# Two graph-attention layers on one core: fewer signals from TensorE, a second set of PSUM banks, deeper rings

## The chip, the core and the metric

One NeuronCore of a Trainium2 chip runs the whole program. The metric is the device time in microseconds, from the start to the end of one execution. The engines are named as in the profile: PE (TensorE matmul; PEld its weight loads), DVE (VectorE), ACT (ScalarE), POOL (GpSimd) and SP (SyncE, which here only issues DMAs). Each runs its own instruction stream, and they wait for each other through semaphores. A "signal" below is an increment of a semaphore that an instruction makes when it completes.

## What is computed

A graph of 6,250 nodes with 128 features and 106,250 edges (100,000 and a loop on each node), sorted by destination. Layer 0 scores each edge by a dot product, layer 1 by an 8-head attention with edge features. What matters of the reference:

```python
# layer 0
qk = x @ Wqk + bqk;  v = x @ Wv + bv
scores = clip(sum(qk[dst] * qk[src], -1) / sqrt(D), -5, 5)
attn = softmax of scores over the edges of one dst
out = segment_sum(attn * v[src], dst) @ Wo + bo      # then residual and norms
# layer 1
z = leaky_relu(xl[src] + xr[dst] + edge_attr @ lin_edge_w.T, 0.2)
alpha = softmax of einsum('ehc,hc->eh', z, att) over the edges of one dst
attn_out = segment_sum(xl[src] * alpha, dst)         # then residual, MLP, norms
```

## The kernel before, in words

The edges are cut into 832 tiles of 128 edges. Four tiles are a quad (208 quads), four quads a group (52 groups). Since edges are sorted by destination, the destinations of a tile lie in a window of 128 consecutive nodes. A gather (a DMA that POOL issues with one row index per edge) fetches the source rows, SP loads the window of the destination table, and one-hot matrices, made by comparing index vectors, spread and collect rows by matmul.

**Layer 0, per quad Q.** SP loads the four windows of `p_tab` and one row of relative indices (`rel_bc`), L253 and L255, into one of SLOTS = 4 slots. POOL issues four gathers (L279) into one of AHEAD0 = 4 slots. DVE makes the one-hot matrix `spread` (L538, ring of 2). PE spreads the window rows in two halves (`spread_p(Q, k)`, L320, two tiles each, into `p_dst0` and `p_dst1`). DVE multiplies them with the gathered rows (`score(Q, k)`, L548) and clips (L566). ACT makes the exponential and the weighted one-hot matrix `gather1` (`weigh`, L438 to L446, ring of 2). PE forms the weighted sums of rows and weights (`add_up(Q, k)`, L330 and L332, two halves, into `tile_sums0` and `tile_sums1`), and DVE adds each tile to `node_sums` (`add_tile`, L560).

The order on each engine is written out by hand. In step T the PE does `spread_p(T+1, 0)`, `add_up(T-1, 0)`, `spread_p(T+1, 1)`, `add_up(T-1, 1)`. Each half ends in a signal of its own: `p_spread` after a half of the spreading, `summed` after a half of the sums, so four in a quad. DVE does `make_spread(T+1)`, then for each half `score(T, k)` and two `add_tile` of quad T-2, then `clip(T)`. SP waits for `p_spread` of quad Q-4 before it loads quad Q, POOL waits for `summed` of quad Q-4 before it gathers quad Q. A PE half waits until DVE has read the same bank of the quad just before (`scored`, `added`). In the first 13 quads the PE also makes blocks of `p_tab` (`make_p`, banks `lr_ps`). From step 204 on the node-wise part of the layer runs beside the last quads (`project`, `turn_y`, `tables`; banks `o_ps`, `t_ps`, `lr_ps`). That is eight PSUM banks in all.

**Layer 1, per quad Q.** SP loads four windows of `xr_tab` (L830), and for each group 1 MB of edge features and the indices. POOL gathers four tiles of `xl_tab` (L846) after it waits for `z_ready` of quad Q-4. PE builds z in one bank (`make_z`): edge features times weights (L905), spread windows (L909), gathered rows (L913), signal `z_ready`. ACT reads it twice (`split_z`, L857 and L858), after waits for `z_ready` and for `lg_ready` of two quads before. PE makes the logits (`make_logits`, L925), signal `lg_ready` in each quad. A softmax over each group follows in small steps on DVE and ACT, with three more PE signals a group. Nine quads later DVE makes messages and one-hot matrices (L1000, L1010), PE collects them (`add_up`, L956), signal `summed`, and DVE adds the tiles (L1022), after a wait for `summed`. In step Q the PE does `make_z(Q+1)`, `make_logits(Q)`, `add_up(Q-10)`.

A last stage does the node-wise MLP. The change does not touch it.

Of the kernel before, what the change touches and what calls it, by code (L numbers as in the profile page):

```python
# [18 lines left out]
BF16 = mybir.dt.bfloat16  # L19
# [5 lines left out]
P = 128  # L25
# [3 lines left out]
QT = 4  # L29
# [15 lines left out]
def build(nc, t, N, E):  # L45
# [37 lines left out]
    AHEAD0 = 4  # L83
    SLOTS = 4
    DENSE = 204
# [5 lines left out]
    def block_tiles(b):  # L91
        return min(QT, dense_tiles - b * QT)

# [4 lines left out]
    with ExitStack() as ctx:  # L98
# [25 lines left out]
        window = sb("window", [P, SLOTS, QT, P + 1])  # L124
        rel_bc = sb("rel_bc", [P, SLOTS, QW], BF16)
        spread = sb("spread", [P, 2, QW])
# [6 lines left out]
        gather1 = sb("gather1", [P, 2, QT, P])  # L133
# [20 lines left out]
        lr_ps = [ps(f"lr_ps{i}", [P, 2, 2 * P]) for i in range(2)]  # L154
        src_in = sem("src_in")
# [21 lines left out]
        window_in = [sem(f"window_in{i}") for i in range(SLOTS)]  # L177
        spread_made = sem("spread_made")
        p_spread = sem("p_spread")
# [6 lines left out]
        summed = sem("summed")  # L186
# [33 lines left out]
        with nc.Block() as block:  # L220
            @block.sync
            def _(sp):
# [22 lines left out]
                for Q in range(quads):  # L245
                    w, s = Q % SLOTS, Q // QUADS
                    if Q >= SLOTS:
                        sp.wait_ge(p_spread, 2 * (Q - SLOTS + 1))
# [20 lines left out]
            def _(pool):  # L269
# [30 lines left out]
            def _(pe):  # L300
# [11 lines left out]
                def spread_p(Q, k):  # L312
                    if k == 0:
                        pe.wait_ge(spread_made, Q + 1)
                        pe.wait_ge(window_in[Q % SLOTS], (Q // SLOTS + 1) * (QT + 1) * DMA)
                    if Q:
                        pe.wait_ge(scored, 2 * (Q - 1) + k + 1)
                    for i in range(2):
                        at = (2 * k + i) * P
                        mm = nc.tensor.matmul(p_dst[k][:, i, 0:P + 1], spread[:, Q % 2, at:at + P],  # L320
                                              window[:, Q % SLOTS, 2 * k + i, :], start=True, stop=True)
                    mm.then_inc(p_spread, 1)

                def add_up(Q, k):
                    if k == 0:
                        pe.wait_ge(onehot_made, Q + 1)
                    if Q:
                        pe.wait_ge(added, (Q - 1) * QT + 2 * k + 2)
                    for i in range(2):
                        nc.tensor.matmul(tile_sums[k][:, i, 0, :], rows[:, Q % AHEAD0, 2 * k + i, :],  # L330
                                         gather1[:, Q % 2, 2 * k + i, :], start=True, stop=True)
                        mm = nc.tensor.matmul(tile_sums[k][:, i, 1, :], ones[:], gather1[:, Q % 2, 2 * k + i, :],  # L332
                                              start=True, stop=True)
                    mm.then_inc(summed, 1)
# [1201 lines left out]
```

## Time and profile before

| | |
|---|---|
| device time, three runs | 2976.26, 2990.29, 2995.08 us (median 2990.29) |
| profiled execution: its own time | 2994.84 us |
| its span in the profile | 2993.0 us (1.8 us lie around it) |
| busy share of the span | PE 74%, PEld 59%, DVE 57%, ACT 38%, POOL 58% |
| mean granted TensorE clock | 0.826 of full speed |
| tiles added by DVE, layer 0 | from 54.6 to 1380.8 us |
| tiles added by DVE, layer 1 | from 1549.3 to 2866.1 us |

The profile is one execution. Its rows give for each group of instructions the busy time, the mean duration and the idle time of the engine just before them, with the engine whose signal ended that idle time; "remote" and "issue" stand there where no recorded event explains it. A timeline lists the instructions of an engine in order of time, with that idle time in brackets. The ends of matmuls are modelled by the profiler, so the gap between the end of a matmul and the start of what waits for it has to be read with that in mind.

### The profile page before, as it was taken

How to read it: one execution, taken by the hardware profiler on the slowest of the kernel's cores; microseconds unless marked ns; L12 is line 12 of the kernel's file. 1: busy time of each engine (PE TensorE's matmuls, PEld its weight loads, DVE VectorE, ACT ScalarE, POOL GpSimd, SP SyncE). 2: the span in 40 equal slices, each digit the busy share in tenths (PEclk: the TensorE clock that was granted, in tenths of full speed). 3: DMA queues.
4: the chain of work that ended last, by engine and by line, in shares of the span. 5: the costliest groups of instructions: out<-in, count | busy, mean ns of one | idle time of the engine just before them, and what ended most of it. 6: DMA issues, size and time to landing. Idle time of an engine off the chain costs nothing. (4 is left out here: it accounts for less than half of the span.)

```text
span 2993.0 us, 52671 instructions
## 1 busy us (share of the span) xinstructions
PE 2201.2 (74%) x14461; PEld 1756.5 (59%) x14461; DVE 1718.3 (57%) x7092; ACT 1126.6 (38%) x2973; POOL 1725.0 (58%) x1739
## 2 busy tenths in 40 slices
PE   7766665666666666667578888887888887888779
PEld 5665665665555666556355555555555665656556
DVE  2355555555555555557346656666666666666766
ACT  2355555555555555555333222222222222222123
POOL 3356666666666666655565656666666666666322
PEclk9687788788788877887788888987888888888879
DMA  5344444444444444432644444444444444444201
GB/s 136 97 117 111 109 112 105 113 113 109 109 111 114 106 112 112 123 88 59 171 148 141 147 142 126 144 143 140 144 146 147 144 131 139 146 146 147 62 20 36
DMA packets 378501, 356.41 MB, mean 119 GB/s; under 512 B 61695, under 2 KB 335743, under 8 KB 371424
## 3 DMA queue, kind: packets, MB, share of 16 engines
q1 hardware_dynamic: 314640, 236.51, 28.3%
q0 software_dynamic: 53248, 109.16, 14.2%
q10 hardware_dynamic: 10320, 7.37, 0.9%
q8 instruction: 118, 1.93, 0.3%
q14 instruction: 175, 1.43, 0.2%
HBM read 338.98 MB, written 13.82 MB: 118 GB/s over the span
## 5 line engine op out<-in xcount | busy, mean ns | idle before, releaser
L846 POOL DMA_INDIRECT rows<-xl_tab,src_cols x832 | 844.0, 1014 | 505.9 <-issue 228.1
L279 POOL DMA_INDIRECT rows<-in_x,src_cols x832 | 796.6, 957 | 537.0 <-issue 208.9
L330 PE MATMUL tile_sums<-gather,rows 128*128 128x128 f32 x1664 | 420.1, 342 | 254.4 <-DVE node_sums L560 172.4
L560 DVE TENSOR_TENSOR node_sums<-node_sums,tile_sums 128x256 f32 x832 | 350.0, 421 | 387.1 <-PE tile_sums L332 182.9
L330 PEld LDWEIGHTS tile_sums<-gather,rows 128*128 128x128 f32 x1664 | 322.9, 241 | 296.7 <-issue 190.1
L320 PE MATMUL p_dst<-window,spread 128*128 128x129 f32 x1664 | 331.1, 333 | 200.9 <-issue 154.1
L1022 DVE SCALAR_TENSOR_TENSOR node_sums<-node_sums,shrunk,tile_sums 128x128 f32 x832 | 280.7, 337 | 238.2 <-remote 175.6
L320 PEld LDWEIGHTS p_dst<-window,spread 128*128 128x128 f32 x1664 | 283.6, 241 | 219.8 <-issue 207.6
L332 PE MATMUL tile_sums<-gather,ones 128*128 128x128 f32 x1664 | 389.8, 323 | 0.0
L548 DVE CUSTOM_DVE_ANT_0 product<-rows,p_dst 128x128 f32<-128x128 f32 x832 | 258.2, 348 | 226.3 <-remote 147.7
L909 PEld LDWEIGHTS z_ps<-spread,window 128*128 128x128 f32 x1664 | 254.6, 221 | 155.2 <-issue 132.9
L446 ACT ACTIVATE gather<-apart,weight,minus 128x128 f32<-128x128 bf16 x832 | 342.6, 482 | 7.0 <-issue 0.2
L332 PEld LDWEIGHTS tile_sums<-gather,ones 128*128 128x128 f32 x1664 | 322.3, 241 | 0.0
L956 PE MATMUL tile_sums<-onehot,message 128*128 128x128 f32 x1664 | 297.8, 327 | 30.7 <-issue 22.5
L857 ACT ACTIVATE z_act<-z_ps,z_bias 128x512 f32<-128x512 f32 x208 | 141.8, 682 | 456.0 <-remote 218.9
L925 PE MATMUL lg_ps<-z_act,att_pad 128*32 128x128 f32 x3328 | 212.3, 299 | 121.6 <-issue 117.4
L956 PEld LDWEIGHTS tile_sums<-onehot,message 128*128 128x128 f32 x1664 | 247.1, 225 | 88.2 <-issue 75.2
L905 PE MATMUL z_ps<-attr,w_e 128*128 128x512 f32 x416 | 272.5, 740 | 12.7 <-issue 12.3
L909 PE MATMUL z_ps<-spread,window 128*128 128x128 f32 x1664 | 262.0, 307 | 13.8 <-issue 11.4
L432 ACT ACTIVATE apart<-iota_row,rel_cols 128x128 bf16<-128x128 f32 x832 | 265.7, 390 | 10.3 <-issue 3.6
L438 ACT ACTIVATE weight<-clipped 128x4 f32<-128x4 f32 x208 | 42.5, 204 | 518.1 <-issue 390.1
L925 PEld LDWEIGHTS lg_ps<-z_act,att_pad 128*32 128x32 f32 x3328 | 104.2, 115 | 208.8 <-issue 202.8
(187 smaller groups left out, 2525.7 us busy)
## 6 DMA issues: line engine op xcount, KB each, us to landing
window<-p_tab SPq DMA_DIRECT2D x832, 64.5 KB
attr<-in_attrT SPq DMA_DIRECT2D x52, 1024.0 KB
window<-xr_tab SPq DMA_DIRECT2D x832, 64.0 KB
rel_bc<-rel_rows SPq DMA_DIRECT2D x208, 128.0 KB
rel_bc<-rel_rows SPq DMA_DIRECT2D x52, 512.0 KB
rows<-in_x,src_cols POOLq DMA_INDIRECT x832
rows<-xl_tab,src_cols POOLq DMA_INDIRECT x832
p_tab<-p_rows ACTq DMA_DIRECT2D x13, 258.0 KB, 3.5
```

The costliest lines, as they stand in the source:

```text
L279: nc.gpsimd.indirect_dma_start(out=rows[:, r, i, :], out_offset=None, in_=t["x"], in_offset=bass.IndirectOffsetOnAxis(ap=src_cols[:, tile: ...
L320: mm = nc.tensor.matmul(p_dst[k][:, i, 0:P + 1], spread[:, Q % 2, at:at + P], window[:, Q % SLOTS, 2 * k + i, :], start=True, stop=True)
L330: nc.tensor.matmul(tile_sums[k][:, i, 0, :], rows[:, Q % AHEAD0, 2 * k + i, :], gather1[:, Q % 2, 2 * k + i, :], start=True, stop=True)
L332: mm = nc.tensor.matmul(tile_sums[k][:, i, 1, :], ones[:], gather1[:, Q % 2, 2 * k + i, :], start=True, stop=True)
L446: o = nc.scalar.activation(gather1[:, Q % 2, i, :], apart[:, i, :], ACT.Relu, bias=weight[:, Q % 2, i:i + 1], scale=minus[:, Q % 2, i:i + 1])
L560: nc.vector.tensor_tensor(span, span, tile_sums[i // 2][:, i % 2, :, :], ALU.add).then_inc(added, 1)
L846: nc.gpsimd.indirect_dma_start(out=rows[:, r, i, :], out_offset=None, in_=xl_tab, in_offset=bass.IndirectOffsetOnAxis(ap=src_cols[:, tile: ...
L905: nc.tensor.matmul(z[:], w_e[:], attr[:, s % 2, at:at + QW], start=True, stop=False)
L909: nc.tensor.matmul(z[:, i * P:(i + 1) * P], window[:, w, i, :], spread[:, Q % 2, i * P:(i + 1) * P], start=False, stop=False)
L925: mm = nc.tensor.matmul(lg_ps[s % 2][lanes, 0, :], att_pad[:, q, :], z_act[:, Q % 2, part, i * P:(i + 1) * P], start=(q == 0 and part == 0 ...
L956: mm = nc.tensor.matmul(tile_sums[Q % 2][:, i, :], message[:, Q % 2, i, :], onehot[:, Q % 2, i, :], start=True, stop=True)
L1022: nc.vector.scalar_tensor_tensor(span, span, shrunk[:, Q // QUADS % 2, 1, tile % CHUNKS:tile % CHUNKS + 1], tile_sums[Q % 2][:, i, :], ALU ...
```

## The change

It does five things.

1. **Layer 0, signals.** `p_spread` and `summed` go. One semaphore `stepped` is incremented once a PE step, by the last matmul of the step. `fetched(Q) = Q + 1` and `added_up(Q) = Q + 3` are the values at which the spreading and the sums of quad Q are done. All of SP, POOL, ACT and DVE wait on it, DVE once for both halves.
2. **Layer 0, banks.** Quads 15, 17, ..., 195 use `o_ps`, `t_ps` and `lr_ps` in place of `p_dst` and `tile_sums`, so that in quads 15 to 196 a PE half waits for the quad two before and not for the one before.
3. **Layer 0, rings.** Gathered rows 4 to 8 slots, windows and `rel_bc` 4 to 6, `spread` and `gather1` 2 to 4.
4. **Layer 1, signals.** `lg_ready` is incremented once a group. `summed` is incremented only in the last 11 quads; before them DVE waits for `z_ready` of a later quad instead, which stands behind the sums on the PE. ACT no longer waits for `lg_ready`.
5. **Layer 1, order.** `add_up(Q-10)` stands ahead of `make_z(Q+1)` in a PE step, not behind `make_logits(Q)`.

```diff
-    AHEAD0 = 4
+    AHEAD0 = 8
+    RING0 = 4
+    SLOTS0 = 6
+    PAIRED = range(15, 196, 2)
+    def same_banks(Q):
+        return Q - (2 if Q in PAIRED or Q - 1 in PAIRED else 1)
+    def fetched(Q):
+        return Q + 1
+    def added_up(Q):
+        return Q + 3
...
+        p_dst2 = [bank[:].rearrange("p (k i) d -> p k (i d)", k=2) for bank in (o_ps, t_ps)]
+        tile_sums2 = [bank[:].rearrange("p i (s d) -> p i s d", s=2) for bank in lr_ps]
...
-                    if Q >= SLOTS:
-                        sp.wait_ge(p_spread, 2 * (Q - SLOTS + 1))
+                    if Q >= SLOTS0:
+                        sp.wait_ge(stepped, fetched(Q - SLOTS0))
...
-                        pool.wait_ge(summed, 2 * (Q - AHEAD0 + 1))
+                        pool.wait_ge(stepped, added_up(Q - AHEAD0))
...
-                    if Q:
-                        pe.wait_ge(scored, 2 * (Q - 1) + k + 1)
+                    if Q and Q != PAIRED[0]:
+                        pe.wait_ge(scored, 2 * same_banks(Q) + k + 1)
+                    bank = p_dst2[k] if Q in PAIRED else p_dst[k]
-                    mm.then_inc(p_spread, 1)
+                    return mm
...
-                        pe.wait_ge(added, (Q - 1) * QT + 2 * k + 2)
+                        pe.wait_ge(added, same_banks(Q) * QT + 2 * k + 2)
-                    mm.then_inc(summed, 1)
+                    return mm
...
                     for k in range(2):
                         if T + 1 < quads:
-                            spread_p(T + 1, k)
+                            mm = spread_p(T + 1, k)
                         if 0 <= T - 1 < quads:
-                            add_up(T - 1, k)
+                            mm = add_up(T - 1, k)
+                    if T <= quads:
+                        mm.then_inc(stepped, 1)
...
-                    dve.wait_ge(p_spread, 2 * Q + k + 1)
                     if k == 0:
+                        dve.wait_ge(stepped, fetched(Q))
...
-                    if i % 2 == 0:
-                        dve.wait_ge(summed, 2 * Q + i // 2 + 1)
+                    if i == 0:
+                        dve.wait_ge(stepped, added_up(Q))
...
-                    if Q >= 2:
-                        act.wait_ge(lg_ready, Q - 1)
...
-                    mm.then_inc(lg_ready, 1)
+                    if q == QUADS - 1:
+                        mm.then_inc(lg_ready, 1)
...
-                    mm.then_inc(summed, 1)
+                    if Q >= UNCOVERED:
+                        mm.then_inc(summed, 1)
...
+                    if Q >= LAG + 1:
+                        add_up(Q - LAG - 1)
                     if Q + 1 < quads:
                         make_z(Q + 1)
                     if Q < quads:
                         make_logits(Q)
-                    if Q >= LAG + 1:
-                        add_up(Q - LAG - 1)
...
+                def wait_sums(Q):
+                    if Q < UNCOVERED:
+                        dve.wait_ge(z_ready, Q + LAG + 3)
+                    else:
+                        dve.wait_ge(summed, Q - UNCOVERED + 1)
```

Where the waits stand is seen on two engines. First the DVE in a step of the middle of layer 0, before; `p_dst0` and `p_dst1` are the two halves of the spread rows, and L560 adds to `node_sums`:

```order
L548 ISA product,scores<-rows,p_dst0 128x128 [waits clip_done,gathered0,p_spread]
...
L560 ISA [waits added,summed]
L560 TENSOR_TENSOR node_sums0<-node_sums0,tile_sums0 128x2x128
...
L548 ISA product,scores<-rows,p_dst1 128x128 [waits p_spread]
...
L560 ISA [waits added,summed]
L560 TENSOR_TENSOR node_sums0<-node_sums0,tile_sums1 128x2x128
...
L566 TENSOR_SCALAR clipped<-scores 128x4 [waits weighted,scored]
```

and the same place now:

```order
L571 ISA product,scores<-rows,p_dst0 128x128 [waits clip_done,gathered0,stepped]
...
L584 ISA [waits added,stepped]
L584 TENSOR_TENSOR node_sums0<-node_sums0,tile_sums0 128x2x128
...
L571 ISA product,scores<-rows,p_dst1 128x128
...
L584 ISA [waits added]
L584 TENSOR_TENSOR node_sums0<-node_sums0,tile_sums1 128x2x128
...
L590 TENSOR_SCALAR clipped<-scores 128x4 [waits weighted,scored]
```

Of the four waits for a PE signal in a step two are left, both on the same semaphore, and the order of the work is unchanged. Second the PE in the middle of layer 1, before:

```order
L925 MATMUL lg_ps1<-z_act,att_pad 32x128 [waits z_split]
L925 MATMUL lg_ps1<-z_act,att_pad 32x128 x7
L956 MATMUL tile_sums1_1<-onehot1,message 128x128 [waits added1,message_made,onehot_made1]
L956 MATMUL tile_sums1_1<-onehot1,message 128x128 x3
L935 MATMUL ends_ps<-ends,lane_head 8x64 [waits shrunk_made,ends_picked]
L905 MATMUL z_ps1<-attr,w_e 128x512 [waits z_split,attr_in1]
L909 MATMUL z_ps1<-spread1,window1 128x128 [waits window_in1_3,spread_made1]
```

and now:

```order
L948 MATMUL lg_ps1<-z_act,att_pad 32x128 [waits z_split]
L948 MATMUL lg_ps1<-z_act,att_pad 32x128 x7
L959 MATMUL ends_ps<-ends,lane_head 8x64 [waits shrunk_made,ends_picked]
L980 MATMUL tile_sums1_0<-onehot1,message 128x128 [waits added1,message_made,onehot_made1]
L980 MATMUL tile_sums1_0<-onehot1,message 128x128 x3
L928 MATMUL z_ps1<-attr,w_e 128x512 [waits z_split,attr_in1]
L932 MATMUL z_ps1<-spread1,window1 128x128 [waits window_in1_3,spread_made1]
```

The cycle of the three kinds of work is the same. The sums follow the logits as before, but are counted to the next step, which is one quad earlier for the same messages, and the small matmuls of the softmax (`ends_ps`) now stand ahead of them.

## Rows read from the trace of the kernel before

**Rows 1.** Head of the page: the whole span.
```profile
span 2993.0 us, 52671 instructions
```
**Rows 2.** Stretches: length, busy us of PE, PEld, DVE, ACT, POOL (instructions), clock, DMA share, GB/s.
```profile
44.00:155.00 111.00, 88.04 (x366) 73.35 (x366) 41.23 (x154) 40.44 (x120) 30.87 (x33) 0.72 0.38 96
155.00:1300.00 1145.00, 738.72 (x4579) 683.40 (x4577) 609.15 (x2663) 633.91 (x1905) 726.86 (x761) 0.81 0.46 112
1550.00:2860.00 1310.00, 1072.85 (x7867) 767.87 (x7865) 846.12 (x3347) 292.84 (x581) 780.50 (x768) 0.85 0.46 136
```
**Rows 3.** Groups with forms, 400 to 1200 us, POOL: busy, mean ns, idle before, releasers.
```profile
L279 POOL DMA_INDIRECT rows<-in_x,src_cols x532 | 508.5, 956 | 292.2 <-issue 133.7 <-remote 102.3 <-PE tile_sums L332 56.2
```
**Rows 4.** Timeline of POOL, layer 0: start us, us, instruction, idle before.
```profile
700.97 0.95 POOL L279 DMA_INDIRECT rows<-in_x,src_cols  x1 [0.30 <-issue]
703.33 0.95 POOL L279 DMA_INDIRECT rows<-in_x,src_cols  x1 [1.40 <-PE tile_sums L332]
...
712.14 0.95 POOL L279 DMA_INDIRECT rows<-in_x,src_cols  x1 [0.30 <-issue]
715.28 0.95 POOL L279 DMA_INDIRECT rows<-in_x,src_cols  x1 [2.19 <-remote]
```
**Rows 5.** Timeline of PE, the same stretch.
```profile
701.32 0.61 PE L320 MATMUL p_dst<-window,spread 128*128 128x129 f32 x4
...
702.66 0.61 PE L320 MATMUL p_dst<-window,spread 128*128 128x129 f32 x4
...
707.24 0.39 PE L332 MATMUL tile_sums<-gather,ones 128*128 128x128 f32 x2
707.47 0.61 PE L320 MATMUL p_dst<-window,spread 128*128 128x129 f32 x4
...
709.56 0.39 PE L332 MATMUL tile_sums<-gather,ones 128*128 128x128 f32 x2
```
**Rows 6.** Timeline of DVE, the same stretch.
```profile
713.37 0.35 DVE L548 CUSTOM_DVE_ANT_0 product<-rows,p_dst 128x128 f32<-128x128 f32 x1 [4.17 <-issue]
...
714.99 0.97 DVE L560 TENSOR_TENSOR node_sums<-node_sums,tile_sums 128x256 f32 x2 [0.98 <-remote]
```
**Rows 7.** Waits, layer 0 (155 to 1300 us): us in total, times, longest.
```profile
PE tile_sums L330 <- DVE node_sums L560: 159.0, 78, 4.1
POOL rows L279 <- remote: 146.9, 79, 2.3
...
DVE node_sums L560 <- PE tile_sums L332: 135.0, 90, 2.6
```
**Rows 8.** Waits, layer 1 (1550 to 2860 us).
```profile
DVE node_sums L1022 <- remote: 166.6, 33, 7.4
...
DVE picked L1146 <- ACT shrunk L873: 153.2, 37, 8.7
...
DVE node_sums L1022 <- PE tile_sums L956: 40.1, 37, 2.7
```
**Rows 9.** Timelines of PE, ACT, POOL and DVE, layer 1.
```profile
2006.63 0.42 PE L913 MATMUL z_ps<-ident,rows 128*128 128x128 f32 x1
...
2010.59 0.60 PE L913 MATMUL z_ps<-ident,rows 128*128 128x128 f32 x4
...
2011.70 1.16 PE L956 MATMUL tile_sums<-onehot,message 128*128 128x128 f32 x8
...
2007.09 0.69 ACT L857 ACTIVATE z_act<-z_ps,z_bias 128x512 f32<-128x512 f32 x1 [1.84 <-PE z_ps L913]
...
2013.58 0.69 ACT L857 ACTIVATE z_act<-z_ps,z_bias 128x512 f32<-128x512 f32 x1 [5.22 <-remote]
...
2007.81 0.96 POOL L846 DMA_INDIRECT rows<-xl_tab,src_cols  x1 [3.85 <-PE z_ps L913]
...
2011.59 0.95 POOL L846 DMA_INDIRECT rows<-xl_tab,src_cols  x1 [0.31 <-issue]
...
2013.93 0.35 DVE L1022 SCALAR_TENSOR_TENSOR node_sums<-node_sums,shrunk,tile_sums 128x128 f32 x1 [0.23 <-PE tile_sums L956]
```

More of the change, by code:

```diff
@@ L123, in build @@
         rows = sb("rows", [P, AHEAD0, QT, P])
[L124 to L126 removed]
+        window = sb("window", [P, SLOTS0, QT, P + 1])
+        rel_bc = sb("rel_bc", [P, SLOTS0, QW], BF16)
+        spread = sb("spread", [P, RING0, QW])
         product = sb("product", [P, QT, P])
@@ L176, in build @@
         gathered = [sem(f"gathered{i}") for i in range(AHEAD0)]
-        window_in = [sem(f"window_in{i}") for i in range(SLOTS)]
+        window_in = [sem(f"window_in{i}") for i in range(SLOTS0)]
         spread_made = sem("spread_made")
-        p_spread = sem("p_spread")
+        stepped = sem("stepped")
         scored = sem("scored")
@@ L326, in add_up @@
                         pe.wait_ge(onehot_made, Q + 1)
[L327 to L328 removed]
+                    if Q == PAIRED[0]:
+                        pe.wait_ge(p_kept, 2 * node_groups)
+                    elif Q:
+                        pe.wait_ge(added, same_banks(Q) * QT + 2 * k + 2)
+                    bank = tile_sums2[k] if Q in PAIRED else tile_sums[k]
                     for i in range(2):
[L330 to L332 removed]
+                        nc.tensor.matmul(bank[:, i, 0, :], rows[:, Q % AHEAD0, 2 * k + i, :],
+                                         gather1[:, Q % RING0, 2 * k + i, :], start=True, stop=True)
+                        mm = nc.tensor.matmul(bank[:, i, 1, :], ones[:], gather1[:, Q % RING0, 2 * k + i, :],
                                               start=True, stop=True)
[L334 removed]
+                    return mm
                 def project(b):
@@ L386, in _ @@
                 spread_p(0, 0)
-                spread_p(0, 1)
+                spread_p(0, 1).then_inc(stepped, 1)
                 for T in range(steps):
@@ L442, in weigh @@
                     act.wait_ge(apart_made, Q + 1)
-                    if Q >= 2:
-                        act.wait_ge(summed, 2 * (Q - 1))
+                    if Q >= RING0:
+                        act.wait_ge(stepped, added_up(Q - RING0))
                     for i in range(QT):
-                        o = nc.scalar.activation(gather1[:, Q % 2, i, :], apart[:, i, :], ACT.Relu,
+                        o = nc.scalar.activation(gather1[:, Q % RING0, i, :], apart[:, i, :], ACT.Relu,
                                                  bias=weight[:, Q % 2, i:i + 1], scale=minus[:, Q % 2, i:i + 1])
@@ L559, in add_tile @@
                     span = node_sums[:, :, bass.ds(base, P)]
-                    nc.vector.tensor_tensor(span, span, tile_sums[i // 2][:, i % 2, :, :], ALU.add).then_inc(added, 1)
+                    bank = tile_sums2[i // 2] if Q in PAIRED else tile_sums[i // 2]
+                    nc.vector.tensor_tensor(span, span, bank[:, i % 2, :, :], ALU.add).then_inc(added, 1)
                 def clip(Q):
@@ L697, in build @@
     ROWS = 16
+    UNCOVERED = quads - LAG - 2
     AHEAD = 4
@@ L997, in send_messages @@
                     if Q >= 2:
-                        dve.wait_ge(summed, Q - 1)
+                        wait_sums(Q - 2)
                     mine = alpha_ps.rearrange("p (k l) -> p k l", k=QT)[:, :, q * HEADS:(q + 1) * HEADS]
@@ L1006, in make_onehots @@
                     if Q >= 2:
-                        dve.wait_ge(summed, Q - 1)
+                        wait_sums(Q - 2)
                     for i in range(QT):
@@ L1016, in add_tile @@
                     if i == 0:
-                        dve.wait_ge(summed, Q + 1)
+                        wait_sums(Q)
                         dve.wait_ge(shrunk_made, Q // QUADS + 1)
@@ L1039, in find_run_max @@
                 def find_run_max(s):
-                    dve.wait_ge(lg_ready, (s + 1) * QUADS)
+                    dve.wait_ge(lg_ready, s + 1)
                     dve.wait_ge(fences_made, s + 1)
```

25 lines of the change are left out of this document (12 added, 13 removed).

## The prediction

> **What bounds the kernel now.** I read the stretches first, then POOL's rows, then the timelines of three engines side by side, last the waits. The middle of layer 0 is 1145 us with 761 gathers [rows 2], that is 190 quads of 6.02 us. No engine is busy for so long: per quad PE has 3.89 us, DVE 3.21, ACT 3.34 and POOL 3.83 (each busy sum of the stretch over 190). POOL is nearest, since a gather takes 0.956 us [rows 3] and 0.30 us lie between two of them [rows 4], so four cost 4 x 1.256 = 5.02 us. The missing 1.00 us a quad are pauses between stretches of gathers: 1.40 us before the one at 703.33, 2.19 us before the one at 715.28 [rows 4]. The eight gathers between them took 9.76 us, so two quads cost 11.95 us, which is 5.98 a quad.
>
> What POOL waits for is the point. The sums it needs at 715.28 ended on PE at 709.56 + 0.39 = 709.95 [rows 5], 5.33 us before. DVE tells the same: its L560 at 714.99 [rows 6] needs the L332 that ended at 707.24 + 0.39 = 707.63 [rows 5] and is 7.36 us late, although DVE idled 4.17 us before 713.37 [rows 6]. POOL's last gather ended at 712.14 + 0.95 = 713.09 [rows 4], and within 2.2 us after it DVE and POOL go on. So I read it thus: **while POOL issues gathers back to back, a signal of PE may be held until they are done**, and POOL then pauses for the signal that its own gathers delayed. The waits agree: POOL's 146.9 us in 79 idle times "remote" [rows 7] are 1.86 us each, with no recorded signal that would explain them.
>
> Layer 1 shows it too, on fewer waits. With POOL idle (3.85 us before 2007.81), z that ended at 2006.63 + 0.42 = 2007.05 is read by ACT at 2007.09, 0.04 us later [rows 9]. In a stretch, z that ended at 2010.59 + 0.60 = 2011.19 is read at 2013.58, 2.39 us later, after the gather that ended at 2012.54 [rows 9]. DVE waits for the sums 166.6 us in 33 idle times "remote" and 40.1 us in 37 with a recorded releaser, and 153.2 us for `shrunk` of ACT [rows 8]. With 846 us busy of 1310 [rows 2] it is the engine that is always either busy or waiting; POOL (780) is not the bound there.
>
> **The change part by part.** The sum is made against the profiled execution, 2994.8 us around a span of 2993.0 [rows 1], which is 4.6 above the median.
>
> *Signals of layer 0.* Four a quad become one, 832 become 210. An increment costs its engine nothing that a row shows: matmuls with and without one read 0.39 us alike [rows 5]. What a removed signal can give is the hold. But the last signal of a step is the one that decides already: after a long stretch all come out together (DVE at 713.37, POOL at 715.28), so one signal comes no earlier than the last of four, except by the time that they take to come out. I take 0 for the signals alone.
>
> *Deeper rings.* POOL may be eight quads ahead of the sums and not four, SP six and not four. It lets a stretch go on if a signal arrived in the meantime. A stretch of twelve gathers is 12 x 0.956 + 11 x 0.30 + 2.19 = 16.96 us, 5.65 a quad in place of 6.02. The ends: nothing, if the ring is full at each stretch (POOL is the slowest engine, so it starts each time with as many free slots as signals let through), and 190 x (6.02 - 5.02) = 190 us, if the pauses go altogether. I take 5.65 for a third of the quads, since POOL is near the bound and a ring that is never full needs the others to be faster: 63 x 0.37 = **-23 us**.
>
> *Banks.* A half step of PE with its pair of spreading and sums is 702.66 - 701.32 = 1.34 us [rows 5]. With one set of banks PE and DVE took turns by halves; now DVE starts when the whole PE step has ended. In the paired quads PE goes on with the next step meanwhile, so I take 0. The 25 quads outside (0 to 14 and 197 to 206) keep one set and the turn is then a whole step: 25 x 1.34 = 34 us if nothing hides it, 0 if `make_p` and the dense part at the end hide it. The first 13 take 111 us for 33 gathers [rows 2], 13.5 us a quad, on PE's chain; between the ends I take the middle, **+17**.
>
> *Start.* POOL can issue eight quads at once, 8 x 5.02 = 40 us where it was 20, while PE builds the first of `p_tab`. If the first signals are held, they come up to 20 us later; that work needs the gathers anyway and partly catches up. Bounds 0 and +15, taken **+5**.
>
> *Layer 1.* 353 signals go: `lg_ready` 208 to 52, `summed` 208 to 11. ACT's wait for `lg_ready` of two quads before was always behind the one for z, 0. DVE's wait for sums turns into one for a later z. In the held case at 2012 the sums ended at 2011.70 + 1.16 = 2012.86, and z 1.67 us before; z came to ACT at 2013.58, the sums to DVE at 2013.93 [rows 9]: 0.35 us. Thus the 33 "remote" waits x 0.35 = 12 us, and the 40.1 us of the 37 others [rows 8] may go too, since the z that is waited for now stands behind sums that DVE wants a step later. Against it: the sums stood behind `make_logits` and now come, with the small matmuls of the softmax, ahead of the next z, so when messages are late PE waits with z as well. I take 7 us for that: 12 + 40 - 7 = **-45**. The ends are 0 and all the waits for sums, -207; what is late next is `shrunk`, 153.2 us [rows 8], which the change does not touch, and that is why I stay near the low end.
>
> The sum is -23 + 17 + 5 - 45 = -46, so 2994.8 - 46 = **2949 us**, 1.4% below the median.
>
> A rule on what signals cost: the Trainium skill, "TensorE: Matmul & The Clock Gate", section "The cost: per-tile semaphore tail", has the increments of concurrent matmuls add about 26.3 ns each to the tail. As an estimate by that page alone, the 975 signals would be worth 26 us at most and the rest of the change nothing, 2969 us. The trace disagrees about what dominates, with a single signal 7.36 us late [rows 5, 6].
>
> **The rivals.**
>
> *B, the pauses mostly go.* Fewer signals and deeper rings let stretches run over four quads: (16 x 0.956 + 15 x 0.30 + 2.19)/4 = 5.50 us. Then 190 x 0.52 = -99, -45, +22: 2873 us. For it: POOL resumed at 703.33 with a 1.40 us pause only, so a signal that is sent early in a stretch does get through. Against: ACT and PE must follow at 5.50 with holds of the size seen.
>
> *C, nothing changes.* The pause after a stretch is set by the hold, not by the number of signals or slots: POOL fills whatever ring it has, then waits for a signal that is held until it stops. Then layer 0 stays at 6.02, the +22 of its ends stand, and of layer 1's 45 half is eaten by the waits for `shrunk`: 2995 us. For it: both stretches shown end in the same way, and the period is 6.0 us for a stretch of eight. This case includes that the banks buy nothing. The Trainium skill, "TensorE: Matmul & The Clock Gate", section "HAM oscillation — how this bites in real kernels", tells of a kernel in which "Adding PSUM double-buffering gave no further gain". As a mechanism here: the bank wait of PE was 159.0 us (78 times) for DVE's L560 [rows 7], and DVE waited 135.0 us for the L332 in turn [rows 7]; both are the same late signals seen from two sides, so taking the bank away moves the wait and ends no earlier. By that the second banks are worth 0, as in the sum.
>
> *D, slower: one signal carries all.* `stepped` frees SP's windows, POOL's slots, DVE's scores and DVE's sums, and it is sent at the end of a step. The loop is: signal, DVE's work of a quad 3.21 us, ACT's 3.34, PE's half step 1.34, over two quads, since the sums of a quad stand one step behind its scores. With 6.02 us a quad the signal may be 12.04 - 7.89 = 4.2 us late before the loop sets the pace. At 5.33 us, as for POOL at 715.28, it gives (7.89 + 5.33)/2 = 6.61 us a quad, +0.59 x 190 = +112. With +22 and -45 that is 3084 us. Before, a half that got through early let part of the work go on; now nothing does. It decides when most signals come over 4.2 us after the end of their step. For it: the two latenesses above lie over that. Against: they are the longest ones, those at the end of a stretch of eight, and PE has a step in reserve now.
>
> **How the numbers follow.** What can be told from no change is about 1%, so faster is below 2960, slower above 3020. My forecast, 2949 with its own range of 2915 to 2980, has a chance of 0.42, B 0.17, C 0.20, D 0.21. Of the forecast's own chance about a quarter lies above 2960, and a little of each side spreads: faster is 0.31 of A and 0.16 of B, together 0.47; within 1% is 0.10 of A and 0.19 of C, 0.29; slower is the rest with D, 0.24. The range reaches from B's 2850 (5.40 a quad) to 3060, inside D, where half of its steps would be late; beyond lie the floor of 2724 (all the pauses, 190 us, and half of layer 1's waits, 103, with the +22) and the whole of D.
>
> **What would show it.** POOL's pause per stretch and the number of gathers in one: more gathers with the same 2.2 us is the forecast, shorter pauses B, 6.0 us a quad C, stretches of four with 2 us D. DVE's waits in layer 0 should stand once a quad and before L548. In layer 1 the waits for `node_sums`, 206.7 us in all, should fall to about 160, and those for `shrunk` stay. The first and the last quads should be longer by some us each. The forecast is wrong if the time of layer 0's middle moves by over 60 us either way, or if layer 1 gains over 100 us because no wait takes the place of those for the sums.

## The result, and the profile after

The changed kernel took 3037.33 us (median of 4 runs, 3027.43 to 3044.97) where the kernel before took 2992.68: a ratio of 1.0147, 95% interval 1.0117 to 1.0176. It was forecast to be 1.4% faster and is 1.5% slower. The profiled executions differ by less, 3027.43 and 2994.84 us, 32.6 us; the rows below explain those 32.6.

The windows of the changed kernel, in the columns of [rows 2]:

```profile
155.00:1300.00 1145.00, 781.53 (x4568) 729.89 (x4567) 592.24 (x2653) 626.52 (x1902) 727.89 (x757) 0.79 0.47 112
1550.00:2860.00 1310.00, 1024.32 (x7806) 745.74 (x7805) 820.76 (x3245) 294.62 (x583) 781.16 (x772) 0.85 0.45 136
```

The additions of DVE bracket the layers. Each row gives the shortest, median and longest duration in ns, then the start of the first and of the last; the third row is layer 1:

```profile
L584 DVE TENSOR_TENSOR node_sums<-node_sums,tile_sums x468: 415/420/425, 78.4 to 1386.7; 128x256 f32 x156
L584 DVE TENSOR_TENSOR node_sums<-node_sums,lr_ps x364: 412/420/424, 209.2 to 1295.9; 128x256 f32 x182
L1054 DVE SCALAR_TENSOR_TENSOR node_sums<-node_sums,shrunk,tile_sums x832: 245/347/351, 1550.5 to 2897.6; 128x128 f32 x167
```

Against 54.6 to 1380.8 and 1549.3 to 2866.1 before, layer 0 starts 23.8 us later and ends 5.9 later, the stretch between the layers is 4.7 shorter, layer 1's additions take 1347.1 us instead of 1316.8 (+30.3), and what follows is 1.1 longer: 5.9 - 4.7 + 30.3 + 1.1 = 32.6. **Layer 1 holds nearly all of it.**

Layer 0's middle kept its period. POOL, with [rows 4] as its partner:

```profile
710.24 0.95 POOL L295 DMA_INDIRECT rows<-in_x,src_cols  x1 [2.23 <-remote]
...
719.14 0.95 POOL L295 DMA_INDIRECT rows<-in_x,src_cols  x1 [0.31 <-issue]
722.25 0.95 POOL L295 DMA_INDIRECT rows<-in_x,src_cols  x1 [2.16 <-remote]
```

Two quads in 722.25 - 710.24 = 12.01 us; over the whole stretch 757 gathers in 1145 us are 6.05 us a quad, where it was 6.02. PE's step ended at 719.25 + 0.63 = 719.88, and DVE went on only at 722.02:

```profile
719.25 0.63 PE L352 MATMUL tile_sums<-gather,ones 128*128 128x128 f32 x2
```
```profile
722.02 0.35 DVE L571 CUSTOM_DVE_ANT_0 product<-rows,p_dst 128x128 f32<-128x128 f32 x1 [5.26 <-remote]
```

The waits of 155 to 1300 us, against [rows 7], say that this repeats: 95 stretches of eight gathers, each with a pause of 203.6/95 = 2.14 us.

```profile
DVE product L571 <- remote: 483.0, 95, 5.4
...
POOL rows L295 <- remote: 203.6, 95, 2.3
```

At the start POOL issues its 32 gathers without a stop, and the signal for the next comes 31.69 us after the last:

```profile
45.38 0.95 POOL L295 DMA_INDIRECT rows<-in_x,src_cols  x1 [0.30 <-issue]
78.02 0.95 POOL L295 DMA_INDIRECT rows<-in_x,src_cols  x1 [31.69 <-PE tile_sums L352]
```

What stood still meanwhile are the first tables. ACT's fourth copy of `p_rows` needs the matmuls that ended on PE at 26.04 + 0.79 = 26.83 us, and starts 2.38 us after POOL's last gather has ended:

```profile
26.04 0.79 PE L325 MATMUL lr_ps<-m_bias,ones 1*128 1x129 f32 x2
48.71 0.37 ACT L445 COPY p_rows<-lr_ps 128x258 f32<-128x258 f32 x1 [19.93 <-remote]
```

This signal is 21.88 us late. SP's first four window loads took 11.93 us beside the same burst, from 26.93 us on, and 2.41 us in the kernel before, whose burst was over by then (SP's timelines).

In layer 1 (1550 to 2860 us) DVE's waits changed places, against [rows 8]:

```profile
DVE picked L1178 <- ACT shrunk L896: 232.6, 42, 10.3
DVE maxima L1122 <- remote: 77.3, 12, 7.3
DVE picked L1178 <- issue: 47.3, 7, 8.4
DVE message L1032 <- remote: 41.5, 12, 4.4
DVE node_sums L1054 <- remote: 39.8, 28, 3.2
DVE node_sums L1054 <- PE z_ps L936: 17.2, 29, 1.3
```

Those for the sums fell from 206.7 us to 57.0, as forecast and by more. But `maxima` and `message`, which each need a small matmul's signal, waited 0.8 us before (L1090, 3 times) and now 77.3 + 41.5 and 13.9 in smaller groups, and `picked` went from 153.2 + 81.7 to 232.6 + 47.3. These windows are equally long and hold more of layer 1 before than now. From the first to the last addition of layer 1 DVE waited 454 us before and 476 now: +22 of the +30.3. Its busy time there is 851 and 853 us; the other 7 us are idle time that the list of waits does not hold. The granted clock does not carry the loss: it is 0.84 before and 0.85 now, and PE is busy for 1077 and 1047 us.

ACT's waits for z grew from 395 to 600 us, though those of ACT in all only from 1008 to 1035. The largest group before and then after:

```profile
ACT z_act L857 <- remote: 190.8, 53, 8.2
```
```profile
ACT z_act L880 <- remote: 320.9, 66, 8.8
```

And PE waits longer for DVE's one-hots, before and then after:

```profile
PE tile_sums L956 <- DVE onehot L1010: 6.9, 7, 2.4
```
```profile
PE tile_sums L980 <- DVE onehot L1042: 42.5, 42, 2.8
```

### The profile page after: what moved, and what is told of

Same layout as the page of the kernel before. It is cut to its first block and busy times, and to the rows that moved or that the text cites. A ratio compares the mean times of both kernels' runs of the same rounds, so it can differ in the third digit from the quotient of the medians.

```text
span 3025.6 us, 52253 instructions
## 1 busy us (share of the span) xinstructions
PE 2200.7 (73%) x14461; PEld 1784.8 (59%) x14461; DVE 1703.4 (56%) x7092; ACT 1119.4 (37%) x2973; POOL 1726.1 (57%) x1739
## 5 line engine op out<-in xcount | busy, mean ns | idle before, releaser
L571 DVE CUSTOM_DVE_ANT_0 product<-rows,p_dst 128x128 f32<-128x128 f32 x468 | 145.4, 348 | 563.5 <-remote 488.2
L337 PE MATMUL p_dst<-window,spread 128*128 128x129 f32 x936 | 222.5, 381 | 251.3 <-issue 227.3
L350 PE MATMUL tile_sums<-gather,rows 128*128 128x128 f32 x936 | 284.4, 402 | 118.4 <-issue 78.1
L337 PEld LDWEIGHTS p_dst<-window,spread 128*128 128x128 f32 x936 | 186.1, 277 | 272.9 <-issue 257.8
L350 PEld LDWEIGHTS tile_sums<-gather,rows 128*128 128x128 f32 x936 | 225.2, 296 | 143.3 <-issue 113.2
L928 PE MATMUL z_ps<-attr,w_e 128*128 128x512 f32 x416 | 263.1, 719 | 11.4 <-DMA attr<-in_attrT 8.6
L352 PE MATMUL tile_sums<-gather,ones 128*128 128x128 f32 x936 | 264.8, 381 | 0.0
L932 PE MATMUL z_ps<-spread,window 128*128 128x128 f32 x1664 | 253.9, 298 | 14.0 <-issue 13.0
L352 PEld LDWEIGHTS tile_sums<-gather,ones 128*128 128x128 f32 x936 | 225.7, 296 | 0.0
L584 DVE TENSOR_TENSOR node_sums<-node_sums,tile_sums 128x256 f32 x468 | 196.5, 420 | 31.6 <-issue 0.7
```

The source lines that it names most:

```text
L337: mm = nc.tensor.matmul(bank[:, i, 0:P + 1], spread[:, Q % RING0, at:at + P], window[:, Q % SLOTS0, 2 * k + i, :], start=True, stop=True)
L350: nc.tensor.matmul(bank[:, i, 0, :], rows[:, Q % AHEAD0, 2 * k + i, :], gather1[:, Q % RING0, 2 * k + i, :], start=True, stop=True)
L352: mm = nc.tensor.matmul(bank[:, i, 1, :], ones[:], gather1[:, Q % RING0, 2 * k + i, :], start=True, stop=True)
L928: nc.tensor.matmul(z[:], w_e[:], attr[:, s % 2, at:at + QW], start=True, stop=False)
L932: nc.tensor.matmul(z[:, i * P:(i + 1) * P], window[:, w, i, :], spread[:, Q % 2, i * P:(i + 1) * P], start=False, stop=False)
```

## The experiments

Five jobs ran, each with the kernel before beside the others. It took 2552.0, 2545.3 and 2546.2 us in the first three (e1 to e4, e5 to e8, e9 to e12) and 2990.9 and 2952.5 in the last two (e13 to e16, e17 and e18). Jobs two and four had the same chip. So the same program on the same chip has two levels, 17.5% apart, and each job is compared within itself. What separates them is in the profiles. In 300 us of layer 0 (e2, whose layer 0 is that of before, and then the kernel before in the first comparison):

```profile
400.00:700.00 300.00, 217.74 (x1415) 203.06 (x1414) 191.53 (x829) 196.77 (x591) 227.72 (x238) 0.86 0.53 131
```
```profile
400.00:700.00 300.00, 193.49 (x1196) 181.11 (x1195) 158.57 (x698) 165.09 (x499) 190.42 (x200) 0.80 0.45 110
```

238 gathers against 200, each of 0.95 us in both. The granted clock differs too, 0.86 and 0.80, but PE is the idler there where the clock is lower (193 us busy against 218), so it does not set the pace. In e2 POOL has no pause at all, and no wait anywhere is "remote". At 2550 us the signals of PE are **prompt**, at 2990 they are **held** while POOL issues; below the jobs are called so. The changed kernel itself ran in a prompt job as e5, and there the copy of `p_rows` that was 21.88 us late follows its matmuls by 0.04 us:

```profile
26.57 0.80 PE L325 MATMUL lr_ps<-m_bias,ones 1*128 1x129 f32 x2
27.41 0.37 ACT L445 COPY p_rows<-lr_ps 128x258 f32<-128x258 f32 x1 [2.53 <-PE lr_ps L325]
```

SP's loads differ too. Near 700 us four window loads took 1.88 to 2.16 us in e2; before, those beside the long stretch of eight gathers took 6.45 us and the ones around it 1.88 to 2.24 (SP's timelines, L255; e2 first):

```profile
706.10 2.16 SPq L255 DMA_DIRECT2D window<-p_tab  x4
```
```profile
705.44 6.45 SPq L255 DMA_DIRECT2D window<-p_tab  x4
```

**The two halves and the whole (prompt).** e1 joins the changed layer 0 to the old layer 1, e2 the old layer 0 to the changed layer 1, e5 is the changed kernel itself.

> Layer 0 as changed, layer 1 as before. Theory: the change of layer 0 costs only its late start and leaves the middle at 6.0 us a quad, so the span grows by 5 to 10 us (about 3000 to 3003), and the layer 1 adds stay at 1317 us. Rival: the loss of the whole change sits in layer 0's slower start and its effects on what follows, then nearly all of the 40 us stay, about 3030.

> Layer 0 as before, layer 1 as changed. Theory: layer 1 alone carries the loss, its adds run 1347 us in place of 1317 and the kernel takes about 3020 to 3030. Rival (the loss is layer 0's): within 5 us of the kernel before.

> The whole change again, beside the kernel before on the same chip. On the chip where the four kernels above ran, the kernel before took 2552 us, POOL issued its gathers in layer 0 without a pause (1.256 us each) and each half of the change gained 0.6%. Theory: what the change is worth depends on whether TensorE's signals are held while POOL issues. Where POOL has no pauses it gains the sum of both halves, 28 to 34 us (2520 beside 2552). Where POOL pauses 2.2 us after each eight gathers (6.0 us a quad) it loses again 1 to 2% (3037 beside 2993). Rival: the two halves hinder each other, so it loses against the kernel before on any chip.

Measured: e1 2535.42, ratio 0.9936 (0.9918 to 0.9954); e2 2537.96, 0.9942 (0.9925 to 0.996); e5 2514.68, 0.9877 (0.9845 to 0.9909). The expectations of e1 and e2 carried the numbers of held signals and fell; e5's theory held. The halves add up, and the same kernel gains 1.2% with prompt signals and loses 1.5% with held ones.

**Parts of layer 1 (prompt).** e3 has the new order alone, e4 the logits' signal alone, e8 the order and the waits for z (with ACT's two waits in the other order). The edits of e3 and e4, shortened:

```diff
 e3, in a PE step of layer 1
+                    if Q >= LAG + 1:
+                        add_up(Q - LAG - 1)
                     if Q + 1 < quads:
                         make_z(Q + 1)
                     if Q < quads:
                         make_logits(Q)
-                    if Q >= LAG + 1:
-                        add_up(Q - LAG - 1)
 e4
-                        act.wait_ge(lg_ready, Q - 1)
...
+                    if q == QUADS - 1:
                         mm.then_inc(lg_ready, 1)
```

> Only the order of the PE in layer 1 is changed (sums ahead of the next z), every signal of before is kept. Theory A, z comes later for ACT and POOL because the sums and their waits for DVE stand before it: this alone gives the loss, +25 to +35 us, about 3020. Theory B, the loss comes from the signals that went (DVE waits for a z that is later than the sums): no loss here, and a gain of up to 20 us is possible since the sums are sent earlier in a step.

> Only the signal of the logits is changed: one a group, and ACT no longer waits for it. Theory A and B both: within 5 us of the kernel before, since ACT's wait for z always ended later. If 156 fewer signals make the others come earlier, it is faster by 10 to 20 us.

> Layer 1 with the new order and with DVE's waits for the sums turned into waits for a later z, the signal of the logits kept in each quad; layer 0 as before. Theory: the order is the whole of it, so this is level with the order alone and with layer 1 alone: 0.994 of the kernel before where signals are prompt. Where they are held, DVE now waits for z in place of the sums, 1.5 us later in PE's order, and it is 10 us or more slower than the order alone, up to the 30 us that layer 1 lost in the first comparison.

Measured: e3 0.9942 (0.9925 to 0.9958), e4 0.9995 (0.9975 to 1.0016), e8 0.9954 (0.9936 to 0.9971). With prompt signals the order is the whole gain of layer 1, and 156 signals fewer are worth nothing that can be measured. In e3 DVE no longer waits for the sums (181.0 us in e4, 1340 to 2400 us), but 73.7 us for `maxima` and 67.6 for `message`, and 61.4 instead of 36.4 for `picked`: the waits move here too, 219 us in sum in e4 and 206 in e3, and a few us are left over.

**The ring of gathers.** e7 is e1 with `AHEAD0 = 4` (prompt). e14 is the kernel before with `AHEAD0 = 8`, e15 and e16 the whole change with 12 and 16 slots (held); to fit, e15 has 5 slots of windows and not 6, e16 has 4, and `spread` and `gather1` have 2 in e16 and not 4.

> Layer 0 as changed but with 4 slots of gathered rows and not 8, layer 1 as before. Theory: the deeper ring brings the late start (POOL's first burst of 32 gathers); with four slots the first tile is added at 55 us and not at 59 (78 where signals are held), and the middle has the same period. So it is level with the run of layer 0 alone or 5 to 20 us faster. Rival, the ring carries layer 0's gain by letting POOL run ahead at the end: it is 10 to 16 us slower than layer 0 alone, level with the kernel before.

> The kernel before with 8 slots of gathered rows in layer 0 and nothing else. Theory: POOL sets the pace of layer 0 from start to end, and four more slots let it issue 16 more gathers while the first tables are made, 16 x 1.256 = 20 us; this alone gives all of layer 0's gain, ratio 0.992 to 0.994 (2530 beside 2546 to 2552). Rival: the ring helps only with the second banks and the single signal, then it is within 5 us of the kernel before.

> The whole change with 12 slots of gathered rows in place of 8 (and 5 slots of windows in place of 6, to fit). If the head start of POOL is the whole of it: another 16 gathers, 20 us less than the whole change, 2495 beside 2546, ratio 0.980. Rival: beyond 8 slots the quads of the start wait for p_tab and PE, not for gathers, so it is level with the whole change, 0.988.

> The whole change with 16 slots of gathered rows (windows 4, spread and gather1 2, to fit). By the head start 40 us less than the whole change, 2475, ratio 0.972; if another engine becomes the bound after the start (the middle then runs at less than 5.02 us a quad until the ring is used up), the gain is less, 2480 to 2500. Rival as for 12 slots: level with the whole change.

Measured: e7 1.0006 (0.999 to 1.0023), so the rival there is right, since e1 gained 0.6% beside its own kernel before: without the ring nothing is left of layer 0's gain. The windows of 0 to 44 us show it as POOL's head start, 37 instructions in e1 and 22 in e7 (the last pair before the clock):

```profile
0.00:44.00 44.00, 30.44 (x94) 21.98 (x95) 9.21 (x30) 5.84 (x16) 30.30 (x37) 1.00 0.68 183
```
```profile
0.00:44.00 44.00, 30.61 (x95) 22.15 (x96) 9.04 (x30) 5.98 (x16) 17.11 (x22) 1.00 0.65 167
```

15 x 1.256 = 18.8 us, and layer 0 ends 1185.1 - 1165.8 = 19.3 us earlier. In the held job the sign turns: e14 1.0056 (1.0027 to 1.0084), e15 1.0195 (1.014 to 1.0251), e16 1.0217 (1.0167 to 1.0267). The longer first burst delays the signals that build the first tables. DVE's additions of layer 0 in e14, e15 and e16:

```profile
L560 DVE TENSOR_TENSOR node_sums<-node_sums,tile_sums x832: 411/422/425, 76.6 to 1388.6; 128x256 f32 x167
```
```profile
L584 DVE TENSOR_TENSOR node_sums<-node_sums,tile_sums x468: 411/420/424, 100.1 to 1401.3; 128x256 f32 x156
```
```profile
L584 DVE TENSOR_TENSOR node_sums<-node_sums,tile_sums x468: 411/420/425, 117.6 to 1419.1; 128x256 f32 x156
```

With 4 slots the first tile of that job is added at 54.8 us. Every four slots more move it by 17 to 24 us, about the length of 16 gathers (20 us). With prompt signals it does not move: 58.2 us with 4 slots (e7) and 58.4 with 8 (e5). In e16 POOL issues its 64 gathers without a stop until 87.85 us, and signals of PE still reach ACT meanwhile, each over 20 us after the one before:

```profile
54.28 0.37 ACT L445 COPY p_rows<-lr_ps 128x258 f32<-128x258 f32 x1 [21.32 <-remote]
77.44 0.37 ACT L445 COPY p_rows<-lr_ps 128x258 f32<-128x258 f32 x1 [22.79 <-remote]
```

So "held until POOL stops" fits the stretches of eight gathers and not a longer one: there a signal gets through late while POOL goes on. The expectations of e14 to e16 were for prompt signals and were not tried: no such job came.

**Without SP's loads (prompt).** e6 is the kernel before, whose SP skips its loads of `rel_bc` and windows from quad 16 on.

> The kernel before, but SP loads no windows and no index rows from quad 16 on in layer 0, so that SP issues nothing there (the spread rows are those of quads 12 to 15). If the pauses of POOL come from SP's loads beside POOL's gathers: on a chip with 6.0 us a quad the period falls to 5.02 and the time by 190 us. If POOL's gathers alone hold the signals: it stays at 6.0. Where the period is 5.02 already, POOL sets it and nothing changes, within 10 us.

Measured: 2540.16 us beside 2545.25, one run, with 240 gathers in 300 us (400 to 700 us) beside 238 in e2. With prompt signals the loads cost nothing that one run can show; whether they take part in holding signals was not tried, since the job had prompt ones.

**Signals late on purpose (prompt).** To have held and prompt signals side by side, SP relays them:

```diff
+                def relay(signal, late):
+                    sp.wait_ge(signal, n)          # the n-th of this signal
+                    sp.dma_start(relayed[0:1, at:at + 1], t["first_dst"][0:1, 0:1]).then_inc(late[...], DMA)
...
-                    act.wait_ge(z_ready, Q + 1)
+                    act.wait_ge(*nth(z_ready_late, Q + 1))
```

and so for each PE signal that POOL, ACT or DVE waits for. e9 is the kernel before with a relay in layer 1, e10 the same with the changed layer 1, which has fewer signals to relay (427 relays, 780 in e9); e11 and e12 have the relay in layer 0, before and changed. In layer 0 SP loads fewer windows ahead at the start, in both.

> The kernel before, with every signal of TensorE in layer 1 made late on purpose: SP waits for it and issues a 4-byte DMA whose completion is what POOL, ACT and DVE wait for (SP's own loads wait for the signal itself). Order of the relays as on PE, so a late one delays those behind it. Expected: each signal about 2 us late or more, DVE waits for the sums grow from 180 us to 300 us or more, the kernel 30 to 150 us slower than before. It is the base for the next run.

> The same lateness with layer 1 as changed (layer 0 as before). Theory: the new layer 1 pays only while signals are prompt; with late ones the waits that it removes come back at the next signal (the maxima, the turned shares, shrunk) and PE waits for DVE's one-hots, so it is level with the late run of before or up to 30 us slower. Rival: fewer signals and sums sent ahead of z help all the more when signals are late, so it is 15 us or more faster than the late run of before, and the loss in the first comparison had another cause.

> The kernel before with the signals of the spreading and of the sums in layer 0 relayed by SP in the same way (four a quad). One set of banks and four slots leave no reserve: the middle of layer 0 goes from 5.0 us a quad to 5.5 to 7, the kernel 80 us or more slower.

> The same relay with layer 0 as changed (one signal a step; layer 1 as before). Theory: the second banks and the deeper rings are worth their place when signals are late by a fixed time: the middle stays at 5.0 to 5.1 us a quad, 60 us or more faster than the late run of before. In the first comparison they were worth nothing, since there a signal was held until POOL stopped, which a deeper ring does not shorten. Rival: one signal that carries all makes it as slow as the late run of before.

Measured: e9 2880.17 (1.1315), e10 3022.81 (1.1902, 1.1859 to 1.1944), against one kernel before of 2546.24. **With late signals the new layer 1 is 143 us slower than the old one; with prompt ones it was 14 us faster.** From the first to the last addition layer 1 takes 1408.0 us in e9 and 1551.1 in e10, which is the 143 us. Both expectations were too mild, and the direction is the theory's. PE's waits for the one-hots, e9 and then e10, from 1340 to 2740 us:

```profile
PE tile_sums L1003 <- DVE onehot L1057: 4.9, 5, 2.4
```
```profile
PE tile_sums L1003 <- DVE onehot L1065: 177.2, 90, 4.8
```

The timelines show what stands behind such a wait. First DVE and PE in e9: while DVE idles 3.63 us for the relay, PE goes through the sums, the small matmul `ends_ps` and the next z without a pause. Then PE in e10:

```profile
1925.10 0.35 DVE L1069 SCALAR_TENSOR_TENSOR node_sums<-node_sums,shrunk,tile_sums 128x128 f32 x1 [3.63 <-DMA relayed<-in_first_dst]
```

```profile
1920.59 1.16 PE L1003 MATMUL tile_sums<-onehot,message 128*128 128x128 f32 x8
1921.67 0.28 PE L982 MATMUL ends_ps<-ends,lane_head 128*8 128x64 f32 x2
1921.88 1.13 PE L952 MATMUL z_ps<-attr,w_e 128*128 128x512 f32 x2
```
```profile
1918.66 0.65 PE L971 MATMUL lg_ps<-z_act,att_pad 128*32 128x128 f32 x16
1923.21 1.79 PE L1003 MATMUL tile_sums<-onehot,message 128*128 128x128 f32 x8 [3.91 <-DVE onehot L1065]
1924.80 1.91 PE L951 MATMUL z_ps<-attr,w_e 128*128 128x512 f32 x2
```

and why DVE was late there: it had waited 3.54 us for `maxima`, the signal of the matmul just ahead of the sums.

```profile
1919.95 0.23 DVE L1145 TENSOR_TENSOR_SCAN maxima<-bars,maxima,ends_ps 8x16 f32<-8x16 f32 x1 [3.54 <-DMA relayed<-in_first_dst]
```

That matmul had ended at 1915.45 us. SP sent its relay only after its own window loads, at 1918.54, so 3.09 of the 4.50 us are SP's queue. The relay is thus a coarse tool: how late a signal is depends on what SP does just then, in e9 and in e10 not at the same places.

After the wait of 3.91 us PE also runs slower, 1.79 us for the eight matmuls that took 1.16 in e9; the granted clock in 1923.2 to 1926.7 us is 0.55, near the lower of its two levels (1.2 and 2.4 GHz). In the whole layer the clock is 0.84 in e9 and 0.82 in e10, and PE's busy time 1021 and 1006 us, so it is not the clock that makes the 143 us. DVE's waits in the layer grow by 140 us: those for the sums fall from 201 to 59 us, those for `maxima` rise from 1 to 154 and those of `picked` for ACT from 335 to 465.

Layer 0 gave little: e11 2588.95 (1.0172, 1.0152 to 1.0193), e12 2585.29 (1.0158, 1.0132 to 1.0184), two runs each. The middle runs at 600/(460/4) = 5.22 and 600/(473/4) = 5.07 us a quad (gathers in 400 to 1000 us). The banks, rings and single signal shorten the middle a little, but the two kernels' times cannot be told apart, where e11 had been expected 80 us or more slower and e12 60 us faster than e11. A relay is less late than a held signal: in e11's timeline the spread rows that PE ended at 698.55 + 0.68 = 699.23 us reach DVE at 703.83, 4.60 us late and 3.08 of them in SP's queue, where the held signal came 7.36 us late [rows 5, 6].

**The order alone, late and held.** e13 and e18 are e9 with the order of e3 and all its signals; e17 is e3 again.

> Layer 0 as before; in layer 1 every signal late as in e9 and e10, all signals of before kept, and only PE's order changed (the sums ahead of the next z). Theory: the order is the cause, since PE now waits for DVE's one-hots with z behind it; the time is that of e10, 3023 us (within 30), and PE's waits for the one-hots stand near 177 us. Rival: the merged signals are the cause (DVE waits for z in place of the sums, the logits come once a group), then this is near e9, 2880 us.

> The new order of layer 1 alone, every signal kept, as in e3. Where the kernel before takes about 2991 us (signals held while POOL issues): by the theory that the order is the cause, 20 to 35 us slower, with the adds of layer 1 at 1340 to 1355 us in place of 1317. By the rival that the merged signals are the cause: within 10 us of the kernel before. Where the kernel before takes about 2550: 0.994 as in e3, and nothing is told.

> The same kernel as e13: the new order with every signal of layer 1 relayed late. Where the kernel before takes about 2550 it stands beside e9 (2880) and e10 (3023): near 3023 the order is the cause of the 143 us between them, near 2880 the merged signals are; in between, both. Where the kernel before takes about 2991, it is again 3275 and nothing is told.

Both jobs had held signals. e13 (1.0943, 1.0876 to 1.101) and e18 (1.1014, 1.0988 to 1.1041) tell nothing on the split. e17 does: 3007.03 beside 2952.45, **1.0182 (1.0159 to 1.0205)**. The order alone costs 55 us there, more than the 20 to 35 expected and no less than the whole change lost (45 us by the medians). Its additions of layer 1 take 1345.8 us, as expected and as in the changed kernel (1347.1). DVE's waits in layer 1 of e17 (1550 to 2860 us):

```profile
DVE maxima L1090 <- remote: 272.4, 38, 9.0
DVE picked L1146 <- ACT shrunk L873: 149.8, 49, 8.4
DVE maxima L1090 <- issue: 25.5, 4, 6.4
DVE message L1000 <- remote: 9.3, 4, 4.3
DVE node_sums L1022 <- remote: 5.7, 4, 1.6
```

All its waits, with 11.2 us of smaller ones, come to 474 us, as in the changed kernel (473) and unlike before (444); over the whole of layer 1 they are 477, 476 and 454. The wait for the sums is gone and stands, larger, at `maxima`.

## Why the prediction was wrong

- *What bounds layer 0, and the hold:* right for this layer. The changed kernel shows 95 stretches with a pause after each, 2.14 us in the mean, and the prompt jobs show what the kernel is without it, 300/(238/4) = 5.04 us a quad. That POOL's gathers are what holds the signals is read from these times; no run with held signals took gathers or SP's loads away. That the hold is not a fixed property, but comes and goes with the job, could not be read from one profile.
- *Deeper rings, -23:* wrong, 0. No stretch grew from eight gathers to twelve; rival C had it, "POOL fills whatever ring it has, then waits for a signal that is held until it stops". A quad took 6.02 us before and 6.05 now.
- *Signals alone, 0, and banks, 0:* not contradicted. No run had the banks alone. The 0.39 us of [rows 5] do not show what an increment costs, since both of these rows end in one. e4 shows 0 for 156 signals of layer 1 where signals are prompt.
- *Start, +5 of at most +15:* wrong in size. The first tile came 23.8 us later, with held signals 20 us for each four slots (e14 to e16). The working had the signals up to 20 us late and then took +5 of at most +15, since the work would catch up; the first tile shows the whole of it. Much is regained later, since POOL is 16 gathers ahead: with the unpaired quads, for which +17 was taken, layer 0 ends 5.9 us later. So layer 0 as a whole comes near the forecast of -23 + 17 + 5 = -1 by luck, since the misses of its terms offset each other.
- *Layer 1, -45:* the step that failed; it measured +30.3. "Against it [...] when messages are late PE waits with z as well. I take 7 us for that" is the term mis-sized. The waits for the sums fell by 150 us (207 to 57), but those for `shrunk`, which were to stay, rose from 153 to 233, `maxima` and `message` came new, and DVE's waits in all grew by 22. The sums of a quad, counted one step earlier, need its one-hots one step earlier, and these stand behind DVE's waits for held signals. That the z behind them is then late for all who read it, and each later signal too, is how the rows are read here; no run tried it by itself. e17 shows that the order is enough for the loss (+55 us), e9 and e10 show the same kernel part 143 us slower with late signals. Whether the merged signals add or give back anything with held signals is open: by the times they would give some 10 us back, by the length of layer 1 (1345.8 and 1347.1 us) nothing, and the two ran in different jobs. Layer 0 alone was not run with held signals either.
- *Rival D* gave the right sign by the wrong mechanism: layer 0's single signal did not slow its middle.
- *The rule on increments:* at 26.3 ns each (the Trainium skill, "TensorE: Matmul & The Clock Gate", section "The cost: per-tile semaphore tail") the estimate was 2969 us, and the 156 signals of e4 would be worth 4 us. e4's interval cannot tell 4 us from nothing, and the measured 3037 us went the other way.

No version was found that beats both kernels whatever the signals do: the change wins with prompt ones, the kernel before with held ones.

## What to carry to other kernels

A wait that was taken away from DVE came back here at the next signal of the same source, where that source's signals were late: sum all waits of the engine from the stage's first to its last instruction, not the one that is removed. Before an engine's order is changed, ask which step's reserve the moved work loses, and what stands behind it in the queue if its input is late. And compare only within a job: the same kernel on the same chip stood at 2545 and at 2991 us, and the sign of this change follows that level.

## What the runs showed of the hardware that was not expected

- With held signals, a matmul's signal reached DVE 7.36 us late [rows 5, 6] and, beside the longest burst of gathers in the changed kernel, ACT 21.88 us late, while POOL's gathers took 0.95 us at both levels. It is not PE's signals alone that suffer: the register instructions that SP carries out before its window loads read 37 to 51 ns each in e2 and 3 to 930 ns in the kernel before, with the same median of 37. Why one job has held signals and another none stayed open; chip, program and input were the same in jobs two and four.
- A gather costs 1.256 us of POOL, issue included, and 237 to 240 in 300 us is what POOL reached with prompt signals in every kernel whose layer 0 had no relay; it has no pause there, and a deeper ring only moves its start.
- A wait on a signal relayed through a 4-byte DMA of SP, SP's queue included, was enough to slow the kernel by 13% in layer 1 (e9) and by 1.7% in layer 0 (e11).
